# Attention and a routed mixture of experts on one core: two chunks of value sums in one burst at steps 3 and 7 of a period, in place of one chunk at every second step

## The chip, the cores and the metric

One NeuronCore of a Trainium2 chip runs the whole kernel. The metric is the device time of one execution in microseconds. Five engines work beside each other: TensorE (PE, the matmuls), VectorE (DVE), ScalarE (ACT), GpSimd (POOL) and SyncE (SP), which issues most DMAs. They meet through semaphores.

## The reference

16 sequences of 512 tokens, 128 features, 16 heads of 8. Attention whose probabilities are mixed half and half with probabilities from which key 0 is taken out, a residual and layer norm, then a top-2 routed mixture of 8 experts (128 to 512 to 128), a residual and layer norm again. Cut to what matters:

```python
scores = einsum('bhqd,bhkd->bhqk', Q, K) / sqrt(8)
probs = softmax(scores)
intervened = probs.at[:, :, :, 0].set(0.0)
intervened = intervened / clip(intervened.sum(-1, keepdims=True), 1e-9, None)
attn_out = einsum('bhqk,bhkd->bhqd', probs + 0.5 * (intervened - probs), V)
x = layernorm(x + attn_out @ Wo.T + bo)
x = layernorm(x + moe(x))        # two experts of eight for each token
```

## The kernel before

**Units and periods.** Attention is cut into units: one sequence b (16 of them) and one group g of four heads (4 groups), 64 units in all. The program runs over periods p, from 12 before the first unit on, each of 8 steps k. b and g of a period are `divmod(p, 4)`. In period p the engines work on several units at once, so that every one has work from another unit:

- `maxima(p + 2, k)` (line 472) on TensorE: two matmuls of 512 queries-by-keys into one of two buffers `mx_ps` (two banks each). VectorE's `maxima` (line 805) reduces it to the largest score of each query. TensorE may write a buffer only when the reduction of two steps before is over (`s_mx_done`).
- `negmax_to_rows(p + 1)` (line 511) at step 1: the maxima are transposed, copied by ScalarE, split by GpSimd and moved by DMA into the rows that the scores' matmul subtracts.
- `scores(p, 2k)` and `scores(p, 2k + 1)` (line 487): one matmul each into one of three banks of a ring (`ring_ps`); ScalarE's `exp_chunk` (line 659) turns it into probabilities of `PT[u % 2]`. A bank is free when the exp of three entries before is over (`s_ring_done`).
- `values(p - 1, c)` (line 497): the value sums over key chunk c (of four). Four matmuls of f32, one for each head, each on its own 32 of the array's 128 columns; the profile has eight records for them. They add up in the bank `acc_ps` from c = 0 to c = 3. c = 0 waits until VectorE has taken the sums of the unit before out of `acc_ps` (`s_acc_drained`), and until all exps of its unit are over. c = 3 raises `s_pv_ready`.
- VectorE's `sums_by_query(p - 2)` (line 814) transposes `acc_ps` at the start of a period, in front of that period's first maxima.

**Work beside.** A table `BEHIND` puts the projections and the other small matmuls of other sequences at fixed steps: at g = 0 `px` (step 5), at g = 1 `v` (3), at g = 2 `wo` (2), at g = 3 `q` (1), `xt` (4), `k` (5) and `gl` (6). Each takes a bank of the ring. VectorE has, behind the maxima of the step: at g = 0 four parts of `route` (steps 1 to 4), at g = 1 `route` (1, 6), `reciprocals` (2) and `attn_to_rows` (7), at g = 2 the statistics of the layer norm (5, 6), at g = 3 its application (1).

**The order on TensorE** is written out by hand (lines 555 to 571): at each step `scores`, `maxima`, `scores`, then the value sums at every odd step, then the rows of maxima and the work of `BEHIND`. The last period's unit has no period behind it: its four chunks stand in the tail (`beside`, line 617), two and two between the expert tiles. Behind attention come 78 expert tiles and a last pass for the second layer norm, neither touched by the change.

The engines' other queues (SP's loads of q and k, GpSimd's splits, normalising, scatters) follow the same periods in their own order, and are not edited.

Of the kernel before, what the change touches and what calls it, by code (L numbers as in the profile page):

```python
# [54 lines left out]
def layer(nc, xT, x, wqT, wkT, wvT, woT, bq, bk, bv, bo, gateT, w1T, w3T, w2T, out):  # L55
# [16 lines left out]
    with ctx:  # L72
# [163 lines left out]
        def is_unit(u):  # L236
            return 0 <= u < UNITS

        def is_seq(b):
            return 0 <= b < NB  # L240
# [222 lines left out]
        def _(pe):  # L463
# [8 lines left out]
            def maxima(u, k):  # L472

                b, g = divmod(u, NG)
                n = STEPS * u + k
                if n >= 2:
                    pe.wait_ge(s_mx_done, n - 1)
                if k == 0:
                    pe.wait_ge(*qk_loaded(u))
                h = HG * g + k // 2  # L480
                for i in range(2):
                    c = 2 * (k % 2) + i
                    last = nc.tensor.matmul(mx_ps[n % 2][:, i, :], QS[b % 2][0:KR, h, P * c:P * (c + 1)],  # L483
                                            KS[b % 2][0:KR, h, :], start=True, stop=True)
                last.then_inc(s_mx_ready, 1)

            def scores(u, i):

                b, g = divmod(u, NG)
                h, c = HG * g + i // QC, i % QC  # L490
                bank = ring_bank("st", u, i)
                if i == 0:
                    pe.wait_ge(s_m_loaded[u % 2], 16 * MR * (u // 2 + 1))
                nc.tensor.matmul(bank, KS[b % 2][0:KR + MR, h, P * c:P * (c + 1)],  # L494
                                 QS[b % 2][0:KR + MR, h, :], start=True, stop=True).then_inc(s_ring_ready, 1)

            def values(u, c):

                b, g = divmod(u, NG)
                if c == 0:  # L500
                    if u > 0:
                        pe.wait_ge(s_acc_drained, u)
                    pe.wait_ge(s_ring_done, ring_at["st", u, 15] + 1)
                    pe.wait_ge(s_v_step, 3 * (b + 1))
                for j in range(HG):
                    last = nc.tensor.matmul(acc_ps[VW * j:VW * (j + 1), 0, :], VE[b % 2][:, c, HG * g + j, :],  # L506
                                            PT[u % 2][:, j, c, :], start=(c == 0), stop=(c == QC - 1))
                if c == QC - 1:
                    last.then_inc(s_pv_ready, 1)

            def negmax_to_rows(u):
                bank = ring_bank("mT", u)
                pe.wait_ge(s_mx_done, STEPS * (u + 1))
                nc.tensor.transpose(bank[0:HG * QC, 0:P], rowmax[u % 2][:, :], ident[:, :])\
                  .then_inc(s_ring_ready, 1)
# [39 lines left out]
            for p in PERIODS:  # L555
                b, g = divmod(p, NG)
                for k in range(STEPS):
                    if is_unit(p):
                        scores(p, 2 * k)
                    if is_unit(p + 2):  # L560
                        maxima(p + 2, k)
                    if is_unit(p):
                        scores(p, 2 * k + 1)
                    if is_unit(p - 1) and k % 2 == 1:
                        values(p - 1, k // 2)
                    if k == 1 and is_unit(p + 1):
                        negmax_to_rows(p + 1)
                    if (g, k) in BEHIND:
                        name, off = BEHIND[g, k]
                        if is_seq(b + off):  # L570
                            behind(name, b + off)
# [826 lines left out]
```

## Time and profile before

| | us |
|---|---|
| median of 3 runs | 1339.41 |
| their lowest and highest | 1336.74, 1347.7 |
| the profiled execution | 1345.57 |
| its span, first to last instruction | 1343.7 |
| TensorE busy | 1274.6 (95%) |
| VectorE busy | 940.4 (70%) |
| ScalarE busy | 830.0 (62%) |
| GpSimd busy | 712.2 (53%) |
| mean granted TensorE clock | 0.968 |

A trace's times are us from the start of the span. A row of the time line is a run of like instructions of one engine: start, length, engine, line, operation, tiles, count, and in brackets the idle time before it with what ended it. Matmuls overlap in the records (a row's length reaches into the next), so TensorE's pace is read from start to start. Attention fills the span up to about 890 us, expert tiles to about 1290, the last pass the rest. TensorE's granted clock is 1.00 at 2.4 GHz and 0.50 at 1.2 GHz.

### The profile page before, as it was taken

To read this page: it belongs to the slowest core of one execution; us is meant where nothing else is said; L and a number is where in the kernel's file an instruction comes from. 1 tells how busy PE (TensorE), PEld (TensorE's weight loads), DVE (VectorE), ACT (ScalarE), POOL (GpSimd) and SP (SyncE) were. 2 spreads that over 40 slices of the span, in tenths; PEclk is the share of its full clock that TensorE was granted. 3 is DMA by queue.
4 is the path that set the end of the run, shared out by engine and by line. 5 is a ranking of instruction groups with operands and counts; after the bars stand their busy time and mean duration, and the time that the engine had idled before them with its cause. 6 is when DMAs were issued, how large, how long until landed. Compare 5 with 4: busy or idle time off the path is not lost.

```text
span 1343.7 us, 22455 instructions
## 1 busy us (share of the span) xinstructions
PE 1274.6 (95%) x7263; PEld 654.0 (49%) x7263; DVE 940.4 (70%) x1591; ACT 830.0 (62%) x1615; POOL 712.2 (53%) x902
## 2 busy tenths in 40 slices
PE   4999999999999999999999999969999999999976
PEld 1233333333333333333333333327999999999952
DVE  7768889899898988988998999934444433333324
ACT  1367767777777777777777777754444444445626
POOL 5123254574554644745745644435787555556546
PEclk9589999999999999999999999979999999999989
DMA  5222222323323232333233233231445333333247
GB/s 144 94 68 73 81 82 78 102 73 105 94 89 97 84 99 81 94 96 95 75 103 105 77 98 115 93 112 26 69 63 95 49 50 50 49 48 42 43 126 259
DMA packets 111394, 116.73 MB, mean 87 GB/s; under 512 B 16688, under 2 KB 90032, under 8 KB 111280
## 3 DMA queue, kind: packets, MB, share of 16 engines
q1 hardware_dynamic: 87472, 97.15, 23.9%
q0 software_dynamic: 23808, 18.14, 9.3%
q8 instruction: 61, 1.00, 0.3%
q14 instruction: 53, 0.43, 0.1%
HBM read 70.34 MB, written 44.83 MB: 86 GB/s over the span
## 4 chain that ended last, share of the span: by engine, by line
PE 71%; DVE 20%; issue 2%; DMA 2%; POOL 2%; SPq 2%; ACT 0%; DVEq 0%; POOLq 0%; ACTq 0%
PE acc_ps L506 13%; DVE rowmax_sb L811 12%; PE mx_ps L483 12%; PE ring_ps L494 11%; PE ring_ps L613 9%; PE mx_ps L587 8%; PE mx_ps L597 8%; DVE TN_sb L820 2%; PE mx_ps L645 1%; PE ring_ps L529 1%; PE ring_ps L523 1%; PE ring_ps L521 1%; PE ring_ps L576 1%; PE ring_ps L545 1%; DVE stats_sb L843 1%
## 5 line engine op out<-in xcount | busy, mean ns | idle before, releaser
L811 DVE TENSOR_REDUCE rowmax_sb<-mx_ps 128x2 f32<-128x1024 f32 x512 | 606.1, 1210 | 90.1 <-PE mx_ps L483 86.1
L662 ACT ACTIVATE probs_sb<-ring_ps 128x512 f32<-128x512 f32 x1024 | 560.5, 598 | 114.5 <-PE ring_ps L494 105.4
L494 PE MATMUL ring_ps<-region_sb 74*128 74x512 bf16 x1024 | 361.5, 388 | 1.5 <-ACT probs_sb L662 1.4
L483 PE MATMUL mx_ps<-region_sb 72*128 72x512 bf16 x1024 | 317.8, 393 | 11.5 <-DVE rowmax_sb L811 8.7
L506 PE MATMUL acc_ps<-probs_sb,values_sb 128*32 128x512 f32 x2048 | 275.0, 610 | 5.4 <-DVE TN_sb L820 5.4
L494 PEld LDWEIGHTS ring_ps<-region_sb 74*128 74x128 bf16 x1024 | 102.4, 101 | 231.5 <-ACT probs_sb L662 134.5
L1165 POOL CAST negmax_parts_sb<-negmax_sb 16x128 bf16<-16x128 f32 x64 | 17.9, 280 | 283.8 <-ACT negmax_sb L668 283.8
L731 ACT ACTIVATE xT_sb<-region_sb 128x512 f32 x78 | 49.1, 630 | 188.1 <-PE mx_ps L597 186.8
L483 PEld LDWEIGHTS mx_ps<-region_sb 72*128 72x128 bf16 x1024 | 97.0, 100 | 131.2 <-DVE rowmax_sb L811 47.5
L1346 POOL DMA_INDIRECT x_d<-probs_sb,values_sb x68 | 106.1, 1561 | 89.6 <-DVE probs_sb L1103 64.8
L1270 POOL DMA_INDIRECT rows_d<-sent_sb,pos_sb x128 | 126.4, 987 | 48.1 <-issue 47.2
L1110 DVE TENSOR_TENSOR probs_sb<-mx_ps,probs_sb 128x1024 f32<-128x1024 f32 (+1 forms) x78 | 84.3, 1080 | 91.5 <-PE mx_ps L597 91.5
L1103 DVE TENSOR_SCALAR probs_sb<-ring_ps,values_sb 128x128 f32<-128x128 f32 x135 | 42.0, 346 | 143.3 <-PE ring_ps L613 143.3
L613 PE MATMUL ring_ps<-region_sb,probs_sb 128*128 x1080 | 137.0, 279 | 3.6 <-DVE probs_sb L1110 3.6
L1346 POOL DMA_INDIRECT y_d<-probs_sb,values_sb x67 | 104.5, 1560 | 65.4 <-DVE probs_sb L1103 54.5
L587 PE MATMUL mx_ps<-k_parts_sb,xT_sb 128*128 128x256 f32 (+1 forms) x624 | 132.2, 355 | 0.5 <-ACT k_parts_sb L736 0.5
L613 PEld LDWEIGHTS ring_ps<-region_sb,probs_sb 128*128 128x128 f32 x1080 | 127.9, 193 | 7.8 <-issue 7.7
L587 PEld LDWEIGHTS mx_ps<-k_parts_sb,xT_sb 128*128 128x128 f32 x624 | 107.9, 192 | 13.7 <-ACT k_parts_sb L736 0.9
L506 PEld LDWEIGHTS acc_ps<-probs_sb,values_sb 128*32 128x32 f32 x2048 | 40.6, 108 | 114.3 <-issue 94.8
L752 ACT ACTIVATE probs_sb<-mx_ps 128x1024 f32<-128x1024 f32 (+1 forms) x78 | 70.4, 903 | 4.6 <-PE mx_ps L587 4.6
L597 PE MATMUL mx_ps<-k_parts_sb,full_q_sb 128*128 128x256 f32 (+1 forms) x312 | 65.4, 353 | 0.0
L597 PE MATMUL mx_ps<-k_parts_sb,full_k_sb 128*128 128x256 f32 (+1 forms) x312 | 65.0, 351 | 0.0
(162 smaller groups left out, 1215.6 us busy)
## 6 DMA issues: line engine op xcount, KB each, us to landing
region_sb<-parts_d SPq DMA_DIRECT2D x384, 96.0 KB
values_sb<-rows_d SPq DMA_DIRECT2D x57, 132.0 KB, 2.2
parts_d<-q_parts_sb SPq DMA_DIRECT2D x16, 384.0 KB, 2.7
parts_d<-k_parts_sb SPq DMA_DIRECT2D x16, 384.0 KB, 2.9
xT_sb<-xT SPq DMA_DIRECT2D x16, 256.0 KB, 3.1
x_sb<-x SPq DMA_DIRECT2D x16, 256.0 KB
x_d<-xn_sb SPq DMA_DIRECT2D x16, 256.0 KB, 3.3
y_d<-padrow_sb SPq DMA_DIRECT2D x16, 256.0 KB, 3.6
```

What stands on the lines that cost most here:

```text
L483: last = nc.tensor.matmul(mx_ps[n % 2][:, i, :], QS[b % 2][0:KR, h, P * c:P * (c + 1)], KS[b % 2][0:KR, h, :], start=True, stop=True)
L494: nc.tensor.matmul(bank, KS[b % 2][0:KR + MR, h, P * c:P * (c + 1)], QS[b % 2][0:KR + MR, h, :], start=True, stop=True).then_inc(s_ring_re ...
L506: last = nc.tensor.matmul(acc_ps[VW * j:VW * (j + 1), 0, :], VE[b % 2][:, c, HG * g + j, :], PT[u % 2][:, j, c, :], start=(c == 0), stop=( ...
L587: last = nc.tensor.matmul(up_ps[:, c, 0:n], W1T[t % 2][:, P * c:P * (c + 1)], XGT[t % 2][:, 0:n], start=True, stop=True)
L597: last = nc.tensor.matmul(lin_ps[:, c, 0:n], W3T[t % 2][:, P * c:P * (c + 1)], XGT[t % 2][:, 0:n], start=True, stop=True)
L613: last = nc.tensor.matmul(y_ps[:, at:at + D], HH[t % 2][:, c, P * w:P * (w + 1)], W2[:, bass.ds(expert + c * D, D)], start=(c == 0), stop= ...
L662: nc.scalar.activation(PT[u % 2][:, i // QC, i % QC, :], ring_bank("st", u, i), ACT.Exp, scale=SCALE).then_inc(s_ring_done, 1)
L752: nc.scalar.activation(SG[t % 2][:, :, 0:n], up_ps[:, :, 0:n], ACT.Silu).then_inc(s_silu, 1)
L811: V.tensor_reduce(rowmax[u % 2][:, 2 * k:2 * k + 2], mx_ps[n % 2][:, :, :], axis=AXX, op=ALU.max, negate=True).then_inc(s_mx_done, 1)
L1110: V.tensor_tensor(HH[t % 2][:, :, 0:n], lin_ps[:, :, 0:n], SG[t % 2][:, :, 0:n], ALU.mult)\
L1270: G.indirect_dma_start(rows_d, bass.IndirectOffsetOnAxis(ap=pos[b % 2][:, s, c:c + 1], axis=0), XE[b % 2][:, c, s, :], None).then_inc(s_sc ...
L1346: G.indirect_dma_start((x1_d, y_d)[t % 2], bass.IndirectOffsetOnAxis(ap=XG[t % RING][:, w, D:D + 1].bitcast(i32), axis=0), YO[t % YRING][: ...
```

## The change

The value sums of a unit's four key chunks no longer stand at steps 1, 3, 5 and 7 of the next period, one each, but two behind each other at step 3 (chunks 0 and 1) and two at step 7 (chunks 2 and 3). Number, shape and order of the matmuls, all waits and all other engines' programs stay as they are.

```diff
                     if is_unit(p):
                         scores(p, 2 * k + 1)
-                    if is_unit(p - 1) and k % 2 == 1:
-                        values(p - 1, k // 2)
+                    if is_unit(p - 1) and k % 4 == 3:
+                        for c in (k // 2 - 1, k // 2):
+                            values(p - 1, c)
                     if k == 1 and is_unit(p + 1):
                         negmax_to_rows(p + 1)
                     if (g, k) in BEHIND:
```

## Rows read from the trace of the kernel before

**Rows 1.** Waits, 200 to 820 us: engine, who, for whom: us, times, longest.

```profile
DVE rowmax_sb L811 <- PE mx_ps L483: 50.4, 70, 1.7
...
PE acc_ps L506 <- DVE TN_sb L820: 4.3, 12, 0.4
```

**Rows 2.** Time line, two steps of g = 2: start, us, engine, line, operation.

```profile
510.27 0.39 PE L494 MATMUL ring_ps<-region_sb 74*128 74x512 bf16 x1
...
510.70 2.23 ACT L662 ACTIVATE probs_sb<-ring_ps 128x512 f32<-128x512 f32 x4 [0.61 <-PE ring_ps L494]
...
511.13 2.36 DVE L811 TENSOR_REDUCE rowmax_sb<-mx_ps 128x2 f32<-128x1024 f32 x2 [0.74 <-PE mx_ps L483]
...
511.80 0.38 PE L494 MATMUL ring_ps<-region_sb 74*128 74x512 bf16 x1
...
512.11 1.07 PE L506 MATMUL acc_ps<-probs_sb,values_sb 128*32 128x512 f32 x8
...
513.11 0.39 PE L494 MATMUL ring_ps<-region_sb 74*128 74x512 bf16 x1
...
513.34 0.60 PE L483 MATMUL mx_ps<-region_sb 72*128 72x512 bf16 x2
```

**Rows 3.** Time line of the tail: the last unit's second pair of chunks.

```profile
908.78 1.92 PE L506 MATMUL acc_ps<-probs_sb,values_sb 128*32 128x512 f32 x16
...
910.63 1.56 PE L587 MATMUL mx_ps<-k_parts_sb,xT_sb 128*128 128x256 f32 x6
```

**Rows 4.** Time line of one period g = 0, TensorE and VectorE.

```profile
530.98 0.39 PE L494 MATMUL ring_ps<-region_sb 74*128 74x512 bf16 x1
...
531.91 2.36 DVE L811 TENSOR_REDUCE rowmax_sb<-mx_ps 128x2 f32<-128x1024 f32 x2
...
536.89 1.22 DVE L811 TENSOR_REDUCE rowmax_sb<-mx_ps 128x2 f32<-128x1024 f32 x1
...
538.80 1.22 DVE L811 TENSOR_REDUCE rowmax_sb<-mx_ps 128x2 f32<-128x1024 f32 x1
...
540.32 3.48 DVE L811 TENSOR_REDUCE rowmax_sb<-mx_ps 128x2 f32<-128x1024 f32 x3
...
541.59 0.61 PE L483 MATMUL mx_ps<-region_sb 72*128 72x512 bf16 x2
...
542.35 1.07 PE L506 MATMUL acc_ps<-probs_sb,values_sb 128*32 128x512 f32 x8
...
543.34 0.39 PE L494 MATMUL ring_ps<-region_sb 74*128 74x512 bf16 x1
```

**Rows 5.** Time line: starts of periods and of their second halves.

```profile
503.18 0.39 PE L494 MATMUL ring_ps<-region_sb 74*128 74x512 bf16 x1
...
515.95 0.39 PE L494 MATMUL ring_ps<-region_sb 74*128 74x512 bf16 x1
...
522.93 0.39 PE L494 MATMUL ring_ps<-region_sb 74*128 74x512 bf16 x1
...
549.12 1.16 PE L529 MATMUL ring_ps<-wv_sb,xT_sb 128*128 128x128 f32 x8
...
550.11 0.38 PE L494 MATMUL ring_ps<-region_sb 74*128 74x512 bf16 x1
...
555.77 0.39 PE L494 MATMUL ring_ps<-region_sb 74*128 74x512 bf16 x1
```

**Rows 6.** Time line, then windows (busy by engine, then clock, DMA share, GB/s).

```profile
187.06 0.60 PE L483 MATMUL mx_ps<-region_sb 72*128 72x512 bf16 x2 [1.19 <-DVE rowmax_sb L811]
...
188.27 1.94 PE L506 MATMUL acc_ps<-probs_sb,values_sb 128*32 128x512 f32 x8 [0.39 <-DVE TN_sb L820]
...
188.00:190.00 2.00, 1.73 (x8) 0.20 (x8) 2.00 (x3) 0.51 (x1) 0.00 (x0) 0.55 0.00 0
...
190.00:192.00 2.00, 2.00 (x11) 0.95 (x8) 0.65 (x2) 0.86 (x2) 0.69 (x2) 0.60 0.00 0
...
862.00:864.00 2.00, 0.90 (x5) 0.21 (x3) 2.00 (x4) 1.43 (x3) 1.26 (x2) 1.00 0.46 137
```

## The prediction

> **What bounds the kernel now.** I read the page first, then the time line of one whole sequence in the middle of attention, then the waits, and last the granted clock around the few long waits of TensorE. The page's busy shares (TensorE 95%, VectorE 70%) say little by themselves, since each of the four periods of a sequence has another load. The waits say more [rows 1]: in the middle of attention TensorE waits for VectorE only a little, and VectorE stands idle 70 times because the next maxima are not there. Both sit near each other's limit, with two `mx_ps` buffers between them.
>
> The time line gives the parts. S is one matmul of `scores`, M one `maxima` (two matmuls), R one reduction of VectorE over an M. S starts, M starts and R starts are read off directly [rows 2]: M starts 0.22 us after an S, R 0.63 after its M, the next S 0.31 before a burst of value sums, and 1.00 us after the burst's start TensorE goes on. From the last S of a step to the first S behind a burst is so 1.31 us, 1.09 more than the 0.22 of an S alone; the S behind it takes 0.23. A burst costs 1.10. R's follow each other every 1.13 us, because three take 3.48 and the last of them 1.22 [rows 4]; exps of ScalarE every 0.54 (four in 2.23 [rows 2]), so 16 of them are 8.7 us of a period of about 13.
>
> A period is 8 steps of S M S, and 8 R plus what VectorE does beside them. The four periods of one sequence take 12.36, 12.43, 12.77 and 15.03 us (g = 0: 530.98 to 543.34; g = 1: to 555.77; g = 2: 503.18 to 515.95; g = 3: to 530.98) [rows 4, 5], 52.6 together. The wait of a burst for `acc_ps`, once a sequence, stands 12 times in 620 us [rows 1], so every 52 us: the pattern repeats. By the code, 11 sequences (b = 2 to 12) have all its parts.
>
> In g = 0 VectorE sets the pace: from 531.91 on its rows stand end to end, 8 R and four parts of `route` between them, and M7 at 541.59 starts 0.05 after the end of R5 (540.32 + 1.22) [rows 4]. In the last half of g = 3 the order is the other way: q, k, gate logits and transposes fill TensorE. The other halves are near balance, with TensorE ahead: steps 4 to 7 of g = 2 take 5.68 (510.27 to 515.95 [rows 2, 5]), which is 16 x 0.215 + 2 x 1.10 = 5.64.
>
> **The change part by part.** *What it saves on TensorE.* No instruction is added or taken away. The 16 matmul records of a pair of chunks in one burst stand in the tail already, with the same tiles: 1.85 us from start to next start (908.78 to 910.63) [rows 3]. One pair now costs 0.09 + 1.85 + 0.01 = 1.95 against 2 x 1.10 = 2.20. Saved: 0.25 us a pair, two pairs a period, 2.0 us a sequence. This is TensorE's own time only.
>
> *What it does to VectorE.* TensorE delivers no M from S7 of a half to the first S of the next: 0.31 + 1.85 = 2.16 us. VectorE holds at most two M's then, and when M3 starts R1 has just ended, so R2 is running and R3 is all that remains. I lay out a half of four steps with nothing beside (t = 0 is its first S): M0 0.23, R0 0.86, R1 1.99, end of R1 3.21; M3 needs that buffer and starts 3.26 (TensorE would be there at 2.8); S 3.69, burst 4.00, end 5.85. Before it was 5.68. VectorE is idle from R3's end (3.12 + 2 x 1.13 = 5.4) to 6.71. So a half without extra work on either engine gets **0.17 us longer**, though its TensorE work got shorter: 5.68 - 0.25 = 5.43 plus 0.42 of waiting.
>
> Now by period, with the extra work of each.
> - g = 0: the transposing of `acc_ps` stands in front of R0, which starts at 0.93 (531.91 - 530.98) [rows 4], so R1's end, M3 and the burst follow later and steps 0 to 3 end at 5.94. M4 starts 6.17, R4 can start at 6.80, but VectorE is busy until 7.82 (538.80 - 530.98) as before. M5 and M6 also stay bound by R3 and R4. So M7 starts where it did, 10.61 (541.59). Before, a burst of 1.00 followed S; now one of 1.85: 10.61 + 0.43 + 0.31 + 1.85 = 13.20 against 12.36: **+0.85**. The time saved at step 3 goes into a wait for M5 to M7.
> - g = 1: steps 0 to 3 end 5.94 + 0.99 (the `v` projection behind the burst, 549.12 to 550.11 [rows 5]) = 6.93, before 6.77 (550.11 - 543.34); steps 4 to 7 5.85, before 5.66: **+0.35**.
> - g = 2: steps 0 to 3 lose the stall in which the first burst waits for `acc_ps` (0.36, the rows of 0.4 [rows 1]), since chunk 0 comes two steps later, but M3 takes that up: 7.02 against 7.09. Steps 4 to 7: 5.85 against 5.68. **+0.10**.
> - g = 3: steps 0 to 3 wait for VectorE with and without the change: between 0 and -0.25, I take -0.10 (near to g = 2). Steps 4 to 7, full of TensorE work, keep the whole -0.25. **-0.35**.
>
> A sequence: +0.85 + 0.35 + 0.10 - 0.35 = **+0.95 us**. Eleven of them: 10.4. Sequences 13 and 14 have no q and k in g = 3, so that period ends near +0.10: 1.4 each, 2.8. Sequences 0 and 1 have no `route` in g = 0, so VectorE sets no pace there and I take 0.35 as in g = 1: 0.45 each, 0.9 for both. In the last, g = 0 and 1 count 1.2; its last two periods have no maxima, and the tail behind them waits in the code for the tile table and the scatter, which VectorE and GpSimd make meanwhile, so I give them 0.3 together: 1.5. Sum 15.6 us.
>
> *What else moves.* No wait is added. `values(u, 0)` waits for `s_acc_drained` and for the last exp, and both are older at step 3 than at step 1. `s_pv_ready` still comes at the end of step 7. The transposing that waits for it fits in 0.8 us in which VectorE has nothing. At steps 1 and 5 `negmax_to_rows` and the work of `BEHIND` have no burst in front of them any more, so the moved maxima of the next unit get about 1 us more slack. ScalarE has three banks when a burst begins, so it stands about 0.9 us at each; with 8.7 us of 13 it catches up, the S's wait for banks less than the M's for R's. The DMA issues of SP and POOL keep their order; their waits are on a unit's last scores and on the splits, whose places in the order stay.
>
> **How the sum stands to the times.** The trace is one execution of 1345.57 us (span 1343.7); the median is 1339.41. The sum is a difference inside attention, so I put it on the median: 1339.4 + 15.6 = **1355.0 us**; a profiled execution would show a span near 1359.
>
> **The rivals.**
> 1. *The saving comes through* (faster). If two buffers covered the longer burst, each pair would give 0.25 us, in 63 periods with two pairs 31 us: 1308 us. For it: TensorE's shares, and that a merged burst was measured. Against it: the layout of the half needs 0.42 us of waiting for R1. It decides at 0.25: if that wait is shorter, halves get shorter than before. Chance 0.07.
> 2. *Gains and stalls nearly cancel.* If only g = 0 loses (it is the one where no buffer enters the argument) and g = 1 gives back what g = 3 gains, a sequence is +0.4 to +0.5, some 7 us: 1346 us. For it: the plain halves differ by 0.17 only, a small difference of long sums. Chance 0.25.
> 3. *The clock falls.* One stretch shows it: TensorE waits 1.19 us for R (187.06) and then 0.39 for `acc_ps`, and the granted clock reads 0.55 and 0.60 over the next 4 us: half speed (1.2 GHz in place of 2.4); the burst takes 1.94 in place of 1.07. Lost: 0.45 x 2 + 0.40 x 2 = 1.7 us [rows 6]. With 1.10 us idle in 2 the clock stayed at 1.00 (862 to 864). After the change the worst stretch is the end of g = 0, with a wait of 0.6 before M6 (TensorE there at 8.5, R4 over at 9.09) and one of 0.7 before M7 (9.95 and 10.61), 1.3 us together within about 3. If most sequences fall there: 12 x 1.7 = 20 us, 1375 us. The Trainium skill (TensorE: Matmul & The Clock Gate, "A second HAM failure mode: psum-queue depth-cycling") says that micro-idles between groups of matmuls, from cycling PSUM banks, can make the clock swing and cost throughput although no single wait is long. The trace so far bears that out once and contradicts it once. Chance 0.20.
> 4. *The switch isn't saved*: the matmuls of a pair cost 2.2 also here. Then each period is another 0.5 longer, less what VectorE's waits cover: about 1371. Against it is the measured 1.85. Chance 0.03.
>
> **Numbers.** My forecast, +0.95 a sequence with 1349 to 1362, has 0.45. About 1% is what a measurement of this kernel can tell from no change; the border for slower is 1352.8. Of the forecast's 0.45 I count 0.12 below it. Faster by over 1%: 0.07 (rival 1). Within 1%: 0.25 + 0.12 = 0.37. Slower: 0.33 + 0.20 + 0.03 = 0.56. The range runs from 1343 (rival 2 with a small clock gain at the start) to 1376 (rival 3); rival 1 lies outside.
>
> **What the changed profile would show.** Bursts x16 in 1.9 us, 1.85 from start to start; if 2.1, rival 4. Start to start of M7 of g = 0 the same, and the period 13.2: if under 12.4, rival 1. VectorE's idle before R in front of M4 and M0 larger: about 1.3 us a burst where it has no extra work. TensorE's waits before M3 and M7 of 0.3 to 0.6 with releaser VectorE. A sequence 53.5 us in place of 52.6. A granted clock of 1.00 in the middle; under 0.97 there, rival 3. No rows of bursts that wait for `TN_sb`. I am wrong if R's pitch changes, or if the order of ScalarE's banks rather than the maxima holds TensorE.

## The result and the profile after

The changed kernel takes 1369.22 us (median of 4 runs, 1365.06 to 1377.29) against 1342.43 us for the kernel before (4 runs, 1336.74 to 1347.7): the ratio is 1.0207, 95% interval 1.0167 to 1.0246. It is slower, by 26.8 us. The profiled execution took 1366.29 us, with a span of 1364.5.

The page of the changed kernel: busy times, the granted clock in 40 slices of the span, and two groups (busy and mean ns of a record, then idle time before it).

```profile
PE 1284.2 (94%) x7263; PEld 660.7 (48%) x7263; DVE 936.0 (69%) x1591; ACT 811.8 (59%) x1615; POOL 714.8 (52%) x902
...
PEclk8799999999999999999899999989999999999989
...
L494 PE MATMUL ring_ps<-region_sb 74*128 74x512 bf16 x1024 | 356.0, 385 | 11.8 <-ACT probs_sb L663 7.7
...
L506 PE MATMUL acc_ps<-probs_sb,values_sb 128*32 128x512 f32 x2048 | 263.1, 634 | 0.0
```

No burst waits any more (0.0 at the end of L506), where twelve bursts waited for `TN_sb` before [rows 1]. Yet TensorE is busy for 1284.2 us, 9.6 more than before, with the same instructions in another order: some of them ran slower.

The waits of the changed kernel, 200 to 820 us (total, times, longest), and the windows of both kernels over the same stretch (busy by engine, then granted clock, DMA share, GB/s):

```profile
DVE rowmax_sb L812 <- PE mx_ps L483: 48.9, 69, 1.6
...
PE mx_ps L483 <- DVE rowmax_sb L812: 5.8, 13, 0.5
```

```profile
200.00:820.00 620.00, 600.39 (x3332) 210.26 (x3332) 531.72 (x816) 424.09 (x869) 332.74 (x480) 0.97 0.29 87
```

The same windows of the kernel before:

```profile
200.00:820.00 620.00, 612.60 (x3495) 211.28 (x3491) 558.88 (x853) 458.30 (x909) 343.10 (x502) 1.00 0.30 92
```

In equal time 3332 matmul records in place of 3495. The clock reads 0.97 here and 1.00 before. The prediction had set "under 0.97" as the mark of its third rival; this is at its edge.

Now one period g = 0 in which the clock holds. It begins at 533.72; the columns are those of [rows 4].

```profile
533.72 0.39 PE L494 MATMUL ring_ps<-region_sb 74*128 74x512 bf16 x1
...
537.82 1.92 PE L506 MATMUL acc_ps<-probs_sb,values_sb 128*32 128x512 f32 x16
...
539.67 0.39 PE L494 MATMUL ring_ps<-region_sb 74*128 74x512 bf16 x1
...
541.58 1.22 DVE L812 TENSOR_REDUCE rowmax_sb<-mx_ps 128x2 f32<-128x1024 f32 x1
...
542.85 0.60 PE L483 MATMUL mx_ps<-region_sb 72*128 72x512 bf16 x2 [0.23 <-issue]
...
543.10 3.48 DVE L812 TENSOR_REDUCE rowmax_sb<-mx_ps 128x2 f32<-128x1024 f32 x3
...
544.37 0.60 PE L483 MATMUL mx_ps<-region_sb 72*128 72x512 bf16 x2 [0.48 <-DVE rowmax_sb L812]
...
545.13 1.92 PE L506 MATMUL acc_ps<-probs_sb,values_sb 128*32 128x512 f32 x16
...
546.98 0.39 PE L494 MATMUL ring_ps<-region_sb 74*128 74x512 bf16 x1
```

The burst at 537.82 is 1.85 from start to next start. M7 starts at 544.37, 10.65 after the period's start (10.61 before), the period takes 13.26 (12.36 before). TensorE's idle time before M6 (542.85) and M7 (544.37) is VectorE's pace showing: M6 waits for R4, which started at 541.58, and M7 for R5, the first of the three from 543.10 on.

And the half that has no extra work on TensorE, steps 4 to 7 of a period g = 2, which the prediction had laid out by start times:

```profile
513.04 0.39 PE L494 MATMUL ring_ps<-region_sb 74*128 74x512 bf16 x1
...
516.32 0.61 PE L483 MATMUL mx_ps<-region_sb 72*128 72x512 bf16 x2
...
517.07 1.92 PE L506 MATMUL acc_ps<-probs_sb,values_sb 128*32 128x512 f32 x16
...
518.93 0.39 PE L494 MATMUL ring_ps<-region_sb 74*128 74x512 bf16 x1
```

The last M of the half stands 3.28 after its start (forecast 3.26), the burst 4.03 (forecast 4.00), and the half ends at 5.89 in this period, at 5.88 in most, where it took 5.67 before.

Last, a period g = 0 that begins at 313.93, in which the clock doesn't hold. First the time line, then three windows of 1 us (the clock is the number before the last two).

```profile
322.45 0.38 PE L494 MATMUL ring_ps<-region_sb 74*128 74x512 bf16 x1
323.05 0.61 PE L483 MATMUL mx_ps<-region_sb 72*128 72x512 bf16 x2 [0.23 <-issue]
323.50 0.60 PE L494 MATMUL ring_ps<-region_sb 74*128 74x512 bf16 x2
324.58 0.60 PE L483 MATMUL mx_ps<-region_sb 72*128 72x512 bf16 x2 [0.48 <-DVE rowmax_sb L812]
...
325.33 3.60 PE L506 MATMUL acc_ps<-probs_sb,values_sb 128*32 128x512 f32 x16
328.87 0.39 PE L494 MATMUL ring_ps<-region_sb 74*128 74x512 bf16 x1
```

```profile
325.00:326.00 1.00, 1.00 (x6) 0.20 (x8) 1.00 (x2) 0.72 (x2) 0.92 (x2) 0.68 0.36 127
326.00:327.00 1.00, 1.00 (x8) 0.19 (x4) 0.78 (x1) 0.04 (x1) 0.94 (x2) 0.50 0.01 4
327.00:328.00 1.00, 1.00 (x12) 0.19 (x4) 0.00 (x0) 0.00 (x0) 0.92 (x2) 0.50 0.00 0
```

Up to M7, 10.65 after the start again, the two periods are alike. The brackets show only the part of a wait behind the modelled end of the row before; from start to start M6 stands 0.60 behind an S that takes 0.22, a wait of 0.38, and M7 1.08 behind two S of 0.44, a wait of 0.64. Four matmuls of 0.22 stand between the two waits: the two of M6 and the two S. In the kernel before, the same M6 starts 0.22 behind its S and M7 (at 541.59 [rows 4]) 0.55 behind two: no wait, and one of 0.11.

```profile
540.38 0.38 PE L494 MATMUL ring_ps<-region_sb 74*128 74x512 bf16 x1
540.60 0.59 PE L483 MATMUL mx_ps<-region_sb 72*128 72x512 bf16 x2
541.04 0.60 PE L494 MATMUL ring_ps<-region_sb 74*128 74x512 bf16 x2
```

In the changed kernel's period from 313.93, the burst behind M7 takes 3.54 from start to start in place of 1.85, the windows read 0.50 (1.2 GHz), and VectorE and ScalarE have nothing from 327 on. The period takes 14.94. That happens in 10 of the 14 periods g = 0 that contain `route` (p = 16, 20, 24, 32, 40, 44, 48, 52, 56 and 60, not 8, 12, 28 and 36); eight lose some 1.65 us, two lose 3.0, because there the half clock lasts into the next period.

The start of the program differs too, but in the other direction, and by no instruction: the first transposing of `acc_ps` (`TN_sb`) starts at 83.99 us before and at 72.47 after. The windows 50 to 78 us show the clock, before (first fence) and after (second):

```profile
50.00:78.00 28.00, 27.96 (x78) 9.57 (x77) 16.60 (x14) 14.29 (x28) 8.33 (x12) 0.50 0.18 57
```

```profile
50.00:78.00 28.00, 26.50 (x138) 8.66 (x138) 25.01 (x23) 21.88 (x44) 11.02 (x17) 1.00 0.21 62
```

The clock rose at 79 us in the profiled execution of before and at 49 in that of after. Up to the first burst of value sums both kernels issue the same instructions, so this is no effect of the change. Among the ten profiled executions whose start no experiment touches (before, after, and eight of the kernels below), the first `TN_sb` starts between 71.8 and 72.5 in four, between 79.6 and 84.0 in six.

The difference of the two traces, measured between starts of `TN_sb` rows:

| | us |
|---|---|
| start, up to the first `TN_sb` (clock's chance) | -11.5 |
| periods 2 to 62: every period's lengthening at full clock | +17.1 |
| ten falls of the clock at the end of g = 0 | +19.0 |
| one fall of before at 187 us [rows 6] that has no counterpart | -3.0 |
| tail | -1.0 |
| sum (spans 1364.5 and 1343.7: +20.8) | +20.6 |

### The profile page after: what moved, and what is told of

Read it like the earlier page. It is cut to its first block, busy times and chain, and to the rows that moved or that the text cites. A ratio compares the mean times of both kernels' runs of the same rounds, so it can differ in the third digit from the quotient of the medians.

```text
span 1364.5 us, 22455 instructions
## 1 busy us (share of the span) xinstructions
PE 1284.2 (94%) x7263; PEld 660.7 (48%) x7263; DVE 936.0 (69%) x1591; ACT 811.8 (59%) x1615; POOL 714.8 (52%) x902
## 4 chain that ended last, share of the span: by engine, by line
PE 66%; DVE 19%; ACT 4%; issue 4%; DMA 2%; POOL 2%; SPq 2%; ACTq 0%; POOLq 0%; DVEq 0%
PE acc_ps L506 15%; DVE rowmax_sb L812 14%; PE mx_ps L483 9%; PE ring_ps L614 9%; PE ring_ps L494 9%; PE mx_ps L588 8%; PE mx_ps L598 8%; ACT probs_sb L663 4%; PE ring_ps L521 1%; PE ring_ps L529 1%; PE ring_ps L523 1%; PE ring_ps L577 1%; PE ring_ps L545 1%; DMA probs_sb<-y_d 1%; PE ring_ps L536 1%
## 5 line engine op out<-in xcount | busy, mean ns | idle before, releaser
L663 ACT ACTIVATE probs_sb<-ring_ps 128x512 f32<-128x512 f32 x1024 | 551.5, 602 | 213.3 <-PE ring_ps L494 186.4
L494 PE MATMUL ring_ps<-region_sb 74*128 74x512 bf16 x1024 | 356.0, 385 | 11.8 <-ACT probs_sb L663 7.7
L483 PE MATMUL mx_ps<-region_sb 72*128 72x512 bf16 x1024 | 315.9, 391 | 20.4 <-DVE rowmax_sb L812 10.6
L506 PE MATMUL acc_ps<-probs_sb,values_sb 128*32 128x512 f32 x2048 | 263.1, 634 | 0.0
L483 PEld LDWEIGHTS mx_ps<-region_sb 72*128 72x128 bf16 x1024 | 85.6, 99 | 152.5 <-DVE rowmax_sb L812 82.9
L506 PEld LDWEIGHTS acc_ps<-probs_sb,values_sb 128*32 128x32 f32 x2048 | 55.4, 113 | 140.6 <-issue 140.2
L821 DVE STREAM_TRANSPOSE TN_sb<-acc_ps 128x512 f32<-128x512 f32 x64 | 45.1, 705 | 53.7 <-PE acc_ps L506 40.1
```

Source lines behind the costliest of these rows:

```text
L663: nc.scalar.activation(PT[u % 2][:, i // QC, i % QC, :], ring_bank("st", u, i), ACT.Exp, scale=SCALE).then_inc(s_ring_done, 1)
```

## The experiments

Each was run beside the kernel before on the same chip. All compute the same outputs by the same value sums; e3, e7, e9, e10 and e11 add matmuls whose results nobody reads. Where the diff has a table, it gives for each step k the chunks that stand there, in the place of the changed condition: the kernel before is `{1: (0,), 3: (1,), 5: (2,), 7: (3,)}`, the change `{3: (0, 1), 7: (2, 3)}`. A fall is a stretch in which the granted clock goes from 1.00 to 0.50; how many there are, and the time of a sequence, are read from the one profiled execution of each kernel.

**e1: the change without g = 0.**

```diff
-                    if is_unit(p - 1) and k % 2 == 1:
-                        values(p - 1, k // 2)
+                    if is_unit(p - 1):
+                        for c in ({1: (0,), 3: (1,), 5: (2,), 7: (3,)} if g == 0 else {3: (0, 1), 7: (2, 3)}).get(k, ()):
+                            values(p - 1, c)
```

> Pairs merged in the periods g = 1, 2, 3; single bursts at steps 1, 3, 5, 7 in g = 0 as before. Theory A (the changed kernel loses in g = 0 twice: the longer last burst stands behind an M7 that VectorE holds back, and TensorE's waits in front of it let the granted clock fall): g = 0 goes back to 12.4 us, the others keep 12.8, 12.85 and 14.8, a sequence is 52.8, no half clock at the end of g = 0, time 0 to 5 us above the kernel before (ratio 1.000 to 1.004). Theory B (long bursts as such starve ScalarE and let the clock fall wherever they stand): three quarters of the loss remain, 20 us, ratio 1.015.

Measured: 1348.24 us against 1343.36, ratio 1.0031 (0.9999 to 1.0063). A sequence takes 53.06, and the clock doesn't fall up to 880 us, near the end of attention. The windows of this kernel:

```profile
200.00:820.00 620.00, 606.91 (x3466) 214.80 (x3463) 551.15 (x844) 439.78 (x899) 340.50 (x498) 1.00 0.30 91
```

Of the change's 2.07% the periods g = 0 alone carry 1.8, by the medians. Six of the eight merged pairs are still there and the clock holds behind all of them, so a long burst alone doesn't bring it down. The 0.46 a sequence over the kernel before is twice what was expected (52.8). Half of it, 0.23, is what g = 1 to 3 lose in the changed kernel as well (+0.39, +0.07, -0.23). The other half is g = 0 itself, which takes 12.60 in place of 12.36 although its bursts stand as before; "What stays open" below says where in the period.

**e2: only the last pair of g = 0.**

```diff
+                        for c in ({1: (0,), 3: (1,), 7: (2, 3)} if g == 0 else {1: (0,), 3: (1,), 5: (2,), 7: (3,)}).get(k, ()):
```

> One pair merged a sequence only: chunks 2 and 3 at step 7 of g = 0; all other bursts as before. Theory A: M7 of g = 0 stays at 10.61 us from the period's start, the period ends at 13.2 in place of 12.36; TensorE waits even longer before M6 and M7 than in the changed kernel, since the first half is shorter, so the clock falls there in most sequences (1.7 to 3 us each). Together 12 us and 15 to 25 us: ratio 1.018 to 1.028, as much as the whole change. Theory B: one merged pair of eight gives an eighth of the loss, 3 to 4 us, ratio 1.003.

Measured: 1381.24 us against 1343.36, ratio 1.0248 (1.0208 to 1.0287). One merged pair out of eight costs at least about as much as all eight together (1.0167 to 1.0246; the intervals overlap). Where the clock holds (two sequences) a sequence takes 53.46, 0.86 more than before; where it falls, 55.1 to 56.8. Here the half clock begins even before M7, and the windows read 0.96:

```profile
446.81 0.63 PE L483 MATMUL mx_ps<-region_sb 72*128 72x512 bf16 x2 [0.23 <-issue]
...
448.33 1.03 PE L483 MATMUL mx_ps<-region_sb 72*128 72x512 bf16 x2
449.16 0.63 PE L494 MATMUL ring_ps<-region_sb 74*128 74x512 bf16 x1
449.72 3.64 PE L506 MATMUL acc_ps<-probs_sb,values_sb 128*32 128x512 f32 x16
```

M7 takes 1.03 in place of 0.60 and the burst 3.64. The clock falls in 12 of the 14 periods g = 0 that contain `route`, with no merged pair elsewhere: the last pair of g = 0 is the place.

**e3: the change, with TensorE's waits at the end of g = 0 filled.** One matmul of 128 columns of f32 before the S of step 6, two before that of step 7, into the bank that this S overwrites.

```diff
+                    if is_unit(p) and g == 0 and k >= 6:
+                        for _ in range(k - 5):
+                            nc.tensor.matmul(ring_bank("st", p, 2 * k)[:, 0:P], ident[:, :], ident[:, :],
+                                             start=True, stop=True)
                     if is_unit(p):
                         scores(p, 2 * k)
```

> The changed kernel with three small f32 matmuls added in each period g = 0 (one in front of the first scores of step 6, two in front of those of step 7, 128 columns each of the bank that the scores then overwrite, some 0.2 us each): they run in time in which TensorE waits for VectorE. If the waits let the clock fall, g = 0 stays 13.25 us in every sequence and the sequences of 55.4 and 56.7 us go: 53.7 each, 15 to 20 us less than the changed kernel, ratio to before 1.008 to 1.012. If the clock falls for another reason (the long burst, or by chance from run to run), nothing goes away: ratio 1.02, or above it by the added work.

Measured: 1354.84 us against 1343.36, ratio 1.0093 (1.0056 to 1.0130). The eleven sequences from p = 10 on take 53.72 to 53.76, a period g = 0 13.26 as in the undisturbed ones above, and no fall is left:

```profile
200.00:820.00 620.00, 608.16 (x3497) 222.20 (x3498) 545.92 (x836) 433.77 (x889) 339.82 (x492) 1.00 0.30 90
```

So work added to TensorE makes the kernel 1.1% faster (1.0207 to 1.0093, two chips). By the medians this splits the change's cost: the lengthening is 0.9% (11.5 us), the clock the rest. The split is rough, since the traces give the lengthening as 17.1 less 1.0 in the tail, and the start alone differs by up to 11.5 us between executions. It also shows that the half clock comes of the waits and not of the long burst, which is still there: 14 of 14 such periods keep the clock, where 4 of 14 did.

**e10: the same filling with other work**, matmuls of 74 rows and 512 columns of bf16, as the scores use.

```diff
-                            nc.tensor.matmul(ring_bank("st", p, 2 * k)[:, 0:P], ident[:, :], ident[:, :],
-                                             start=True, stop=True)
+                            nc.tensor.matmul(ring_bank("st", p, 2 * k), KS[b % 2][0:KR + MR, HG * g, 0:P],
+                                             QS[b % 2][0:KR + MR, HG * g, :], start=True, stop=True)
```

> As the filled changed kernel (one matmul in front of step 6, two in front of step 7 of g = 0), but each filler is a bf16 matmul of 74 rows and 512 columns like those of scores, about 0.22 us each, in place of an f32 one of 128 columns and about the same time. If any work in the waits keeps the clock, g = 0 is 13.26 us in all sequences as with f32. If it wants f32 work on all rows, the falls come back in part or in full: sequences of 55.4 and 56.7 between those of 53.7, 1365 us.

Measured: 1357.42 us (one run; the kernel before had 1336.68 beside it), the same eleven sequences 53.70 to 53.72, no fall. One run can't be compared in time, and its start was a late one (first `TN_sb` at 82.44); the trace is what counts here. In this trace TensorE's fillers and the burst behind them, at full clock:

```profile
384.58 0.59 PE L560 MATMUL ring_ps<-region_sb 74*128 74x512 bf16 x2
...
386.20 1.92 PE L506 MATMUL acc_ps<-probs_sb,values_sb 128*32 128x512 f32 x16
```

The type of the filler's work does not matter here; that the wait is filled does.

**e4: merged pairs only where they were forecast to gain**, the first of g = 2 and both of g = 3.

```diff
+                        for c in ({0: {1: (0,), 3: (1,), 5: (2,), 7: (3,)}, 1: {1: (0,), 3: (1,), 5: (2,), 7: (3,)}, 2: {3: (0, 1), 5: (2,), 7: (3,)}, 3: {3: (0, 1), 7: (2, 3)}}[g]).get(k, ()):
```

> Pairs merged only where the changed kernel got shorter: steps 0 to 3 of g = 2, both halves of g = 3; the rest as before. Theory A: g = 0 12.36, g = 1 12.43, g = 2 12.64, g = 3 14.80, a sequence 52.2 in place of 52.6, 5 to 6 us less in all: ratio 0.996 (0.993 to 0.999). Theory B: three merged pairs of eight lose 8 to 10 us, ratio 1.007.

Measured: 1362.64 us against 1343.36, ratio 1.0129 (1.0093 to 1.0165). A clear miss: expected was a small gain. The time line of this kernel's g = 2, first half:

```profile
401.06 0.39 PE L494 MATMUL ring_ps<-region_sb 74*128 74x512 bf16 x1
...
404.44 0.60 PE L483 MATMUL mx_ps<-region_sb 72*128 72x512 bf16 x2 [0.76 <-DVE rowmax_sb L812]
...
406.95 1.92 PE L506 MATMUL acc_ps<-probs_sb,values_sb 128*32 128x512 f32 x16
408.81 0.39 PE L494 MATMUL ring_ps<-region_sb 74*128 74x512 bf16 x1
```

The half takes 7.75, where the changed kernel has 6.96 with the same steps 0 to 3. What differs is the second half of g = 1, in front of it: in e4 it ends as early as before, so g = 2 begins while VectorE still has R7, `attn_to_rows` and the transposing in front of R0. R0 ends at 3.36, and M2, which needs its buffer, stands at 3.38. By the bracket that is a wait of 0.76, from start to start one of 0.94 (1.16 behind an S of 0.22, which starts at 403.28). With single bursts chunk 0 at step 1 covers that time; merged, nothing does. In the changed kernel the longer last burst of g = 1 covered it. And that one wait went with a fall of the clock in 6 of 13 sequences (14.7 us between two `TN_sb` instead of 13.09). My halves had been costed from t = 0 as if VectorE came into each of them free of old work.

**e6: e4 with the last pair of g = 1 merged as well**, the test of that explanation.

```diff
-  1: {1: (0,), 3: (1,), 5: (2,), 7: (3,)}
+  1: {1: (0,), 3: (1,), 7: (2, 3)}
```

> As the kernel merged in g = 2 and g = 3, with the last pair of g = 1 merged too. In that kernel the first half of g = 2 took 7.75 us where 6.96 was expected: VectorE carries R7, two transposes and R0 over from g = 1, and the burst at step 1 that covered this had moved to step 3. If that is the cause, a longer burst at the end of g = 1 gives VectorE the time instead: g = 1 12.62 (was 12.43), first half of g = 2 6.96, no wait of 0.76 before M2 and no fall of the clock there, a sequence 52.4 to 52.6, ratio 0.998 to 1.002. If the merged pair of g = 2 itself is the cause, g = 2 stays at 7.75 and the kernel at 1.013 or more.

Measured: 1341.62 us against 1342.32, ratio 0.9985 (0.9947 to 1.0023). One more merged pair brings 1.4%. The first half of g = 2 takes 6.96, the fall is gone (13.09 each time), and the windows read 1.00:

```profile
200.00:820.00 620.00, 611.07 (x3488) 216.25 (x3481) 555.89 (x855) 449.22 (x906) 346.48 (x504) 1.00 0.30 92
```

Of the eleven sequences two take 52.43 and nine 52.64 to 52.77, against 52.60 before. So neither the times nor this trace show a gain. The nine differ from the two in g = 0 alone (12.57 to 12.70 in place of 12.36), as in e1.

**e8: chunks 0 and 1 merged everywhere**, 2 and 3 single.

```diff
+                        for c in {3: (0, 1), 5: (2,), 7: (3,)}.get(k, ()):
```

> Only the pairs of steps 1 and 3 merged, in all periods; bursts at steps 3 (two chunks), 5 and 7. By theory A with what the kernel merged in g = 2 and 3 showed: g = 0 12.4 to 12.6 (the chain that holds M7 is not longer, and a single burst follows), g = 1 12.6, first half of g = 2 7.75 in place of 7.10 with a wait of 0.8 before M2, g = 3 15.0: a sequence 53.3 to 53.6 where the clock holds, and falls of the clock in g = 2 in place of the end of g = 0.

Measured: 1354.51 us (one run, 1342.32 before beside it), a sequence 53.45 with the clock holding, as forecast, and falls in g = 2 in 4 of 13 sequences (and once in g = 3), after the wait that e4 had shown:

```profile
395.83 0.60 PE L483 MATMUL mx_ps<-region_sb 72*128 72x512 bf16 x2 [0.77 <-DVE rowmax_sb L812]
```

g = 0 has no falls: its first pair is harmless, its last is the one that counts.

**e5: all four chunks at step 7**, the same mechanism at double size.

```diff
+                        for c in range(QC) if k == 7 else ():
+                            values(p - 1, c)
```

> All four chunks behind each other at step 7, so 3.56 us in one burst (1.00 + 3 x 0.85). By the layout of theory A: M7 of g = 0 is held back by the same chain of VectorE and stays at 10.6 us, the period ends at 10.61 + 0.74 + 3.56 = 14.9 where the clock holds (before 12.36, changed kernel 13.25). A period without extra work: R's every 1.13 from 0.93, M7 at 7.85, end at 12.15 (before 11.45, changed kernel 11.83). In front of the burst TensorE waits more, so a clock that falls there makes g = 0 longer still by up to 3.5 us. Theory B, by length of burst alone, would give the same excess in every period.

Measured: 1465.31 us (one run, 1342.32 before beside it), mean clock 0.905. Periods 2 and 4, which have little beside, take 12.19 (forecast 12.15). But g = 0 with `route` takes 16.9 to 18.5 and never the 14.9 that the layout gives, because its clock fell in every sequence. One such period begins at 281.16:

```profile
286.47 0.61 PE L483 MATMUL mx_ps<-region_sb 72*128 72x512 bf16 x2 [0.92 <-DVE rowmax_sb L812]
...
288.38 1.03 PE L483 MATMUL mx_ps<-region_sb 72*128 72x512 bf16 x2 [0.87 <-DVE rowmax_sb L812]
...
293.87 5.79 PE L506 MATMUL acc_ps<-probs_sb,values_sb 128*32 128x512 f32 x32
```

The brackets before M4 and M5 read 0.92 and 0.87. M5 already runs at half clock (1.03), M7 starts at 11.29 in place of the 10.6 of the layout, and the burst takes 5.8 in place of the 3.57 from start to start seen at full clock. With no burst between the maxima TensorE has less to do while VectorE reduces, so it waits longer than in the changed kernel, and here the clock fell in 14 of 14 periods.

**e7: the start filled once.** Three f32 matmuls of 512 columns on the older `xT`, ahead of the wait for that of sequence 2 (about 38 us), in the kernel before.

```diff
                 if name == "q":
+                    for _ in range(3 if b == 2 else 0):
+                        nc.tensor.matmul(bank, wq_sb[:, :], xT_sb[1][:, :], start=True, stop=True)
                     pe.wait_ge(s_xT[b % 2], 16 * (b // 2 + 1))
```

> The kernel before with three f32 matmuls of 128 x 512 added in front of the wait for the input of sequence 2, at some 38 us, where TensorE has nothing to do for 2.2 us; they write the bank that the projection then overwrites. In the trace of the kernel before the clock is at half from 28 to 78 us, in that of the changed kernel only to 49, and the first units end 11.4 us earlier there. If steady f32 work lifts the clock, it is at 1.00 from about 45 us on in every run: cost up to 2.4 us, gain up to 11, median 3 to 8 us below the kernel before, ratio 0.994 to 0.998. If not, 2.4 us more: ratio 1.002.

Measured: 1338.32 us against 1342.32, ratio 0.9972 (0.9939 to 1.0004): unclear. The clock is up from 41 to 51 us, at half until 68, then up again; the first `TN_sb` comes at 77.52, between the two cases of the untouched start. It did half of what it was meant to do.

**e11: the kernel before with the start filled twice**, as e7 and with two f32 matmuls of 128 columns before each maxima of steps 2 to 7 in period -1.

```diff
+                    if p == -1 and k >= 2:
+                        for _ in range(2):
+                            nc.tensor.matmul(acc_ps[:, 0, 0:P], ident[:, :], ident[:, :], start=True, stop=True)
                     if is_unit(p + 2):
                         maxima(p + 2, k)
```

> The kernel before with both fillers of the start, and no merged pair. It splits the 0.9964 of the last kernel. In its trace a sequence took 52.44 us, in those of the kernel before and of the one with three fillers 52.6 to 52.8: the merged pairs would be worth 0.2 to 0.3 us a sequence, 2 to 5 us. If so, this kernel lies at 0.998 to 1.000 of the kernel before with a small spread (its lowest runs no lower than those before). If the whole gain is the start's, 0.996 again.

Measured: 1334.05 us (12 runs, 1331.82 to 1336.63) against 1336.73 (1333.01 to 1347.61), ratio 0.9973 (0.9951 to 0.9995), between the two cases expected. The first `TN_sb` at 72.85, a sequence 52.60. The runs lie within 4.8 us of each other, those of the kernel before on the same chip within 14.6.

**e9: e6's table and both fillings of the start**, the version that the rest pointed to.

> The schedule of the kernel merged in g1's last pair, g = 2 and g = 3, with the three f32 matmuls in front of the input of sequence 2, and two f32 matmuls of 128 columns in front of each maxima of steps 2 to 7 of the last period before the first unit, in the bank of the value sums, which nobody uses yet. With the first three alone the clock was at 1.00 from 41 to 51 us and fell again behind waits of 0.89, 0.53, 0.36 and 0.31 us at 44 to 50 us. If the waits are what lets it fall, it now holds from 42 us on: first units as early as in the best traces (first transposing at 71 to 73 us), every run near the lowest ones of the kernel before: median 1333 to 1337, ratio 0.992 to 0.997. If the start is ruled by something else, 0.998 to 1.001.

Measured: 1332.30 us (12 runs, 1329.91 to 1334.08) against 1336.68 (1331.56 to 1343.35), ratio 0.9964 (0.9944 to 0.9983). It is faster than both kernels. The first `TN_sb` is at 72.69, a sequence takes 52.43. Its windows at the start and in the middle:

```profile
50.00:78.00 28.00, 26.78 (x141) 8.73 (x139) 25.40 (x23) 22.20 (x44) 10.76 (x16) 1.00 0.23 72
```

```profile
200.00:820.00 620.00, 612.79 (x3500) 216.74 (x3492) 556.55 (x859) 453.10 (x909) 346.59 (x504) 1.00 0.30 92
```

Against e11, which differs by the merged pairs alone, the intervals overlap. That these pairs bring anything stands only in the traces: 0.17 us a sequence, some 2 us in all.

## Why the prediction was right and wrong

It said slower, 1355.0 us, with 1343 to 1376 as its range. Measured were 1369.2: 26.8 us more than before, where the sum had 15.6. The direction and most steps held. The size missed because the sum held nothing for the granted clock.

| step | forecast | measured |
|---|---|---|
| merged burst, start to start | 1.85 | 1.85 |
| plain half (steps 4 to 7 of g = 2), before and after | 5.68 and 5.85 | 5.67 and 5.88 |
| M7 of g = 0 after its period's start | 10.61 | 10.65 |
| g = 0 | +0.85 | +0.89 |
| g = 1 | +0.35 | +0.39 |
| g = 2 | +0.10 | +0.07 |
| g = 3 | -0.35 | -0.23 |
| a sequence at full clock | +0.95 | +1.12 |
| attention at full clock, all sequences | +15.6 | +17.1 (periods 2 to 62) |
| falls of the clock | left out; as rival 12 x 1.7 = 20, chance 0.20 | 10 falls, 19.0 |

**What held.** That a pair saves 0.25 of TensorE's time, and that two buffers of maxima give it back as a wait: a plain half got 0.21 longer, forecast 0.17. That M7 of g = 0 stays where VectorE puts it, so that the burst's extra 0.85 stands behind it in full. No burst waits for `TN_sb`. ScalarE's banks hold TensorE for 0.2 at step 2 of a period, as small as assumed. Rivals 1, 2 and 4 fall: no half of g = 0 or g = 1 got shorter, a sequence at full clock is +1.12 and not +0.4, and a pair is 1.85. On the saving, the Trainium skill (TensorEngine Tiling (Array Packing), "Key Properties") says that changing the tiling mode drains TensorE; one change of mode to and from the value sums less for each merged pair is what would be saved. The trace agrees in sign, at 0.25 us a pair; no run here separates the drain from the rest of it.

**The term that was mis-sized.** In g = 3 the first half gave 0.03, where I took 0.10 between bounds of 0 and 0.25, and the second 0.20 in place of 0.25. With 0.04 more in g = 0 and g = 1 each that makes 1.12 for 0.95, and 17.1 for 15.6: 1.5 us of the miss.

**The step that failed** is the term for the granted clock at the end of g = 0: the sum put it at nothing and left it to rival 3, "The clock falls". The runs showed 19.0 us in its place in the profiled execution, and e3, with the waits filled, has a ratio of 1.0093 in place of 1.0207. Its place (the waits before M6 and M7 of g = 0), its price (1.7 each) and its sum (20) were all in the prediction and came out as about 1.65 in eight places and 3.0 in two. What was wrong was the chance of 0.20, drawn from two stretches of before: a fall after waits of 1.19 and 0.39 us, and none after 1.10 us idle in 2 [rows 6]. I took 1.3 us in pieces to be more likely safe than not. The changed kernel shows the clock falling after pieces of 0.38 and 0.64 us between matmuls, 1.0 together and so even less than forecast, in 10 of 14 places that are laid out alike. e2 has falls in 12 of the same 14 places, e4 and e8 show them after a single piece of 0.9, and e3 and e10 that they go when it is filled. The Trainium skill (TensorE: Matmul & The Clock Gate, "A second HAM failure mode: psum-queue depth-cycling") has it that micro-idles between groups of matmuls can make the clock swing; the trace agrees, at 19 us here. I had cited that against one row for and one against. And every sequence offers the same pieces: the question was not whether one stretch falls, but how many of a dozen do. If only a quarter of them had been counted (5 us), the forecast would have moved by a third.

**The sum against the medians.** With 17.1 and 19.0, less the tail's 1.0, the changed kernel would stand 35 above one whose clock never falls in attention, and 32 above the profiled one of before if both had the same start. The medians differ by 26.8, the lowest runs by 28.3. Which of the two starts each of the unprofiled runs had, and how many of its sequences fell, isn't known, so the 5 us between are not assigned to a cause. The prediction put its difference on the median and not on the profiled time, which was sound: the profile of before had the late start.

**What stays open.** Why four of fourteen like places keep the clock. Whether a third maxima buffer would turn the saved 0.25 into a gain, as the layout suggests: it wasn't tried.

Also, why g = 0 takes 0.2 more in most sequences of e1, e6 and e7 and in many of e4. e7 merges nothing and shows it too (a sequence 52.80), so it does not come of the merged pairs. The traces show where it arises: ScalarE copies the bank of `px` 0.75 to 0.8 us after its matmuls, rarely up to 1.16, in place of 0.04, the S of step 7 waits for that bank, and M7 stands 0.22 later. First the copy in the kernel before (its period begins at 478.38), then copy and S in e7 (471.21):

```profile
487.98 0.22 ACT L700 ACTIVATE prefix_sb<-ring_ps 128x64 f32<-128x64 f32 x1 [0.96 <-PE ring_ps L550]
```

```profile
481.54 0.22 ACT L702 ACTIVATE prefix_sb<-ring_ps 128x64 f32<-128x64 f32 x1 [1.69 <-PE ring_ps L494]
...
481.82 0.39 PE L494 MATMUL ring_ps<-region_sb 74*128 74x512 bf16 x1 [0.17 <-ACT prefix_sb L702]
```

What holds ScalarE back there isn't shown. e1 and e4 ran on one chip and e6 and e7 on another; e9 and e11, on two others, have the copy at 0.04 every time. So the chip is not ruled out as a cause, and e6 and e9, the same table of merged pairs, should not be compared with each other in tenths of a microsecond.

## What to carry to other kernels

Putting bursts together saves what stands between them, but the engine that feeds from the other buffers must live through the longer burst: lay out one cycle by start times, with each consumer's old backlog in it, before counting the saving. Where the layout leaves TensorE in waits of half a microsecond that repeat in every cycle, look at the granted clock, and put it into the sum rather than beside it. If such waits can't be removed, a few matmuls that nobody needs can fill them: here three in each period g = 0 left it at 13.26, as long as where the clock held without them, and gave back more than 1%.

## What the runs showed of the hardware

- Short waits of TensorE were enough for half clock: 0.38 and 0.64 us with four matmuls between (10 of 14 places in the changed kernel), or one of 0.94 (6 of 13 sequences in e4). Price, from the starts of `TN_sb`: 1.65 us, or 3.0 where it lasts into the next period.
- Three matmuls of 0.2 us each in the waits held the clock at 1.00 in 14 of 14 places, f32 (e3) and bf16 (e10, one run) alike.
- The same instructions at the start led to a rise of the clock at 49 us in one execution and at 79 in another, 11.5 us of difference. From 50 to 78 us of the later one TensorE was busy for 27.96 of 28.00 us at 0.50: a full record of busy time did not by itself bring the clock up. Two fillings of the start (e9, e11) brought the runs from within 11.8 and 14.6 us to within 4.2 and 4.8.
